# Attention scores as float32r products on the two halves of TensorE's rows

## The reference, cut to what matters

```python
N_HEAD = 16                                   # nh; hs = C // nh = 16
k_eff = (W_dq.T @ W_uq.T @ W_uk).reshape(nh, hs, n_kvl)
c_kv = x @ W_dkv.T
q = (x @ W_dq.T @ W_uq.T).reshape(B, T, nh, hs)
q_lat = jnp.einsum('bqhd,hdl->bhql', q, k_eff)
attn = jnp.einsum('bhql,bkl->bhqk', q_lat, c_kv) / sqrt(hs)
attn = jnp.where(causal[None, None], attn, -jnp.inf)
attn = jax.nn.softmax(attn, axis=-1)
y_lat = jnp.einsum('bhqk,bkl->bhql', attn, c_kv)
y = jnp.einsum('bhql,hld->bqhd', y_lat, v_eff)
```

## Time and profile before

| | before |
|---|---|
| median of 3 runs (lowest, highest) | 1285.98 us (1284.98, 1291.69) |
| the profiled execution | 1286.14 us |
| its span | 1284.0 us |
| PE busy | 91% |
| DVE busy | 67% |
| ACT busy | 52% |
| POOL busy | 30% |
| granted clock of PE, mean | 0.969 |

### The profile page before, as it was taken

One profiled execution on the slowest core, in us unless ns is written; L12 is line 12 of the kernel. 1 busy time (PEld: TensorE's weight loads), 2 busy tenths in 40 slices (PEclk: granted clock), 3 DMA queues, 4 the chain that ended last, 5 costly groups with the idle time before them and its releaser, 6 DMA issues.

```text
span 1284.0 us, 32364 instructions
## 1 busy us (share of the span) xinstructions
PE 1166.2 (91%) x13250; PEld 717.1 (56%) x13250; DVE 857.1 (67%) x2072; ACT 662.6 (52%) x1449; POOL 391.0 (30%) x614
## 2 busy tenths in 40 slices
PE   6889999999999999998799997768899778899995
PEld 3334444444434444433688885436676666688884
DVE  6686868777788888871563367797867563465255
ACT  4446666676666666666432237745554222342232
POOL 5421414141300000002333125645564223643210
PEclk9899999999999999999899998989999999999998
DMA  6754425454564444400000000102111110000003
GB/s 205 165 138 51 88 30 95 59 90 61 90 121 51 51 51 51 51 3 2 1 1 1 1 26 15 31 9 57 38 37 32 40 30 12 3 1 1 1 9 123
DMA packets 78755, 61.65 MB, mean 48 GB/s; under 512 B 41360, under 2 KB 65552, under 8 KB 78480
## 3 DMA queue, kind: packets, MB, share of 16 engines
q1 hardware_dynamic: 77456, 57.18, 24.8%
q10 hardware_dynamic: 1152, 2.41, 0.6%
HBM read 38.20 MB, written 20.97 MB: 46 GB/s over the span
## 4 chain that ended last, share of the span: by engine, by line
PE 32%; DVE 10%; issue 5%; POOL 3%; ACT 1%; DMA 0%; POOLq 0%; DVEq 0%; SPq 0%
PE psum L1044 8%; PE psum L1050 7%; PE psum L1059 2%; PE psum L1588 2%; PE psum L1528 2%; DVE d_products L1725 2%; DVE d_inverse L1730 2%; PE psum L1566 2%; DVE d_conv_sum L1800 1%; PE psum L1557 1%; PE psum L1523 1%; PE psum L1510 1%; PE psum L1514 1%; PE psum L257 1%; PE psum L1537 1%
## 5 line engine op out<-in xcount | busy, mean ns | idle before, releaser
L751 ACT ACTIVATE weights<-psum 128x512 f32<-128x512 f32 (+1 forms) x608 | 318.3, 584 | 156.9 <-PE psum L652 154.8
L652 PE MATMUL psum<-q_stack,k_stack 99*128 99x512 bf16 (+3 forms) x768 | 224.0, 328 | 1.8 <-ACT weights L751 1.0
L574 PE MATMUL psum<-k_stack,q_stack 96*128 96x512 bf16 (+3 forms) x768 | 209.2, 328 | 5.3 <-DVE maxima L809 2.0
L809 DVE TENSOR_REDUCE maxima<-psum 128x1 f32<-128x512 f32 (+2 forms) x304 | 189.2, 683 | 12.5 <-PE psum L574 11.9
L806 DVE CUSTOM_DVE_ANT_0 unread<-psum,mask_scores 128x384 bf16<-128x384 f32 (+1 forms) x256 | 159.5, 623 | 50.3 <-PE psum L574 26.8
L669 PE MATMUL psum<-weights,v_rows 128*17 128x512 f32 (+3 forms) x1536 | 162.0, 494 | 0.1
L545 POOL TENSOR_TENSOR residual<-residual,att_o 128x256 f32<-128x256 f32 x32 | 23.3, 727 | 350.0 <-DVE att_o L842 350.0
L1044 PE MATMUL psum<-f_xT,f_weights_hi 128*128 128x512 f32 x384 | 122.9, 402 | 4.2 <-DVE f_hidden L1160 2.1
L652 PEld LDWEIGHTS psum<-q_stack,k_stack 99*128 99x128 bf16 x768 | 72.6, 98 | 90.1 <-ACT weights L751 41.3
L1086 ACT ACTIVATE f_gates<-psum,ffn_biases 128x512 f32<-128x512 f32 x72 | 49.5, 689 | 140.4 <-PE psum L1050 132.6
L1128 DVE TENSOR_TENSOR f_state<-f_gates 128x512 f32<-128x512 f32 x32 | 27.2, 849 | 116.5 <-POOL f_gates L1003 73.8
(11 more groups left out here) (168 smaller groups left out, 2238.8 us busy)
## 6 DMA issues: line engine op xcount, KB each, us to landing
qk_parts<-a_parts SPq DMA_DIRECT2D x32, 384.0 KB, 3.6
q_stack<-qk_parts SPq DMA_DIRECT2D x90, 128.0 KB, 6.6
k_stack<-qk_parts SPq DMA_DIRECT2D x90, 128.0 KB, 7.3
residual<-in_x SPq DMA_DIRECT2D x8, 512.0 KB, 7.4
out_x<-residual SPq DMA_DIRECT2D x8, 512.0 KB, 3.0
ffn_weights<-in_ffn_w ACTq DMA_DIRECT2D x1, 2048.0 KB, 11.7
systems<-d_attnT_k_kb_v SPq DMA_DIRECT2D x32, 64.0 KB, 1.8
d_systems<-systems SPq DMA_DIRECT2D x4, 512.0 KB, 3.5
```

The source lines that it names most:

```text
L574: m = e.matmul(out[:, i * width:(i + 1) * width], self.qst[st][0:self.ROWS, h, qb * P:(qb + 1) * P], self.kst[st][0:self.ROWS, h, k0:k0 + ...
L652: m = e.matmul(out[:, j * width:(j + 1) * width], self.kst[st][0:self.ROWS + self.MAX_ROWS, h, kb * P:(kb + 1) * P], self.qst[st][0:self.R ...
L751: e.activation(self.weights[n % 2][:, heads[0]:heads[-1] + 1, 0:width], bank[self.score_bank[n, i]][:, 0:len(heads) * width].rearrange("p ...
L809: e.tensor_reduce(to, scores.rearrange("p (h x) -> p h x", h=len(heads)), AXIS_X, ALU.max, negate=True).then_inc(*s["max_red"].did(u, w_at))
```

## The change

Queries and keys are split in two float32r parts instead of three bf16 ones, and three products of them (hi hi, lo hi, hi lo) make a stack of 3 x 16 = 48 rows. Two heads of a unit stand on partitions 0 to 63 of a stack, the other two on 64 to 127, so a head's matmul uses one half of PE's rows. The two halves write different banks. The negated maximum has two parts (50 rows in the second making), and four DMAs. ACT writes hi, DVE (early groups) or POOL (later ones, from a raw copy by ACT) subtracts; the other splitting operations are gone.

A piece for the maxima now takes two adjacent banks, one per half, and DVE reduces both by one instruction: 20 pieces per unit. Every piece and every step on the diagonal is masked on PE, by two bf16 matmuls of 64 rows and 64 columns per head and half; the custom DVE instruction is gone. Scores of one step alternate between the halves (heads 0, 2, 1, 3), steps of 128 columns are two scores of two heads instead of one of four, `mixed` keeps the two of a pair side by side. Scores have banks 0, 1, 6, the ring is 2 to 5, `LEAD` is 6.

```diff
-    SPLIT = ((0, 1, 0, 1, 2, 0), (0, 0, 1, 1, 0, 2))
-    PRODUCTS, ROWS, MAX_ROWS = 6, 6 * HS, 3
-    LEAD = 8
-    PROLOGUE_BANKS, SCORE_BANKS, RING = (0, 1, 2, 3, 4, 5, 6), (0, 1, 2), (3, 4, 5, 6)
+    SPLIT = ((0, 1, 0), (0, 0, 1))
+    PRODUCTS, ROWS, MAX_ROWS, ONES_FROM = 3, 3 * HS, 2, 32
+    HALF, PER_HALF = P // 2, HPU // 2
+    LEAD = 6
+    PROLOGUE_BANKS, SCORE_BANKS, RING = (0, 1, 2, 3, 4, 5, 6), (0, 1, 6), (2, 3, 4, 5)
...
-            self.qst = [sb(f"q_stack{i}", [P, HPU, T], BF16) for i in range(STACKS)]
+            self.qst = [sb(f"q_stack{i}", [P, self.PER_HALF, T], F32R) for i in range(STACKS)]
...
-                n = min(HPU, BANK // width)
-                self.pairs += [(qb, c, width, range(h, h + n)) for h in range(0, HPU, n)]
+                alone = width * self.PER_HALF > BANK
+                self.pieces += [(qb, c, width, heads) for heads in (((0, 2), (1, 3)) if alone else ((0, 1, 2, 3),))]
...
+        self.scored = [((0, 1), (2, 3)) if self.span(n)[1] * self.PER_HALF <= BANK else ((0,), (2,), (1,), (3,))
+                       for n in range(len(self.steps))]
...
+                    size = 2 if item[0] == "max" else 1
+                    while size == 2 and (ring[at % len(ring)] % 2 or ring[at % len(ring)] + 1 not in ring):
+                        at += 1
...
+    def mask(self, e, out, mask, h, heads, width, at):
+
+        k, rows = self.k, self.in_stack(h, self.HALF)[0]
+        columns = out[:, 0:heads * width].rearrange("p (h x) -> p h x", h=heads)
+        for n in range(2):
+            e.matmul(columns[:, :, at + n * self.HALF:at + (n + 1) * self.HALF], k.masks16[rows, mask, n, :],
+                     k.ident16[rows, rows].rearrange("p (o x) -> p o x", o=1).to_broadcast([self.HALF, heads, self.HALF]),
+                     start=n == 0, stop=False, skip_group_check=True)
...
+                for half in range(2):
+                    n = self.PER_HALF * QB
+                    for r in range(self.MAX_ROWS):
+                        row = half * self.HALF + self.ROWS + r
...
+                for half in range(2):
+                    rows, out = self.in_stack(half * self.PER_HALF, self.ROWS)[0], bank[self.bank[item] + half]
+                    if diagonal:
+                        self.mask(e, out, 0, half * self.PER_HALF, each, width, width - P)
+                    for i, h in enumerate(heads[half * each:(half + 1) * each]):
+                        j = h % self.PER_HALF
+                        m = e.matmul(out[:, i * width:(i + 1) * width], self.qst[st][rows, j, qb * P:(qb + 1) * P],
+                                     self.kst[st][rows, j, k0:k0 + width], start=not diagonal and i == 0, stop=True,
+                                     skip_group_check=True)
...
+            for i, h in enumerate(heads):
+                rows, j = self.in_stack(h, self.ROWS + self.MAX_ROWS)
+                m = e.matmul(out[:, i * width:(i + 1) * width], self.kst[st][rows, j, kb * P:(kb + 1) * P],
+                             self.qst[st][rows, j, q0:q0 + width], start=not self.diagonal(n) and i == 0, stop=True,
+                             skip_group_check=True)
...
-                if self.ends_on_diagonal(self.pairs[w_at])[1]:
...
-                    e.tensor_tensor_reduce(self.unread[:, 0:width], scores, k.later16[:, BANK - width:BANK], -1.0, HIGH, ALU.add,
-                                           ALU.min, to).then_inc(*s["max_red"].did(u, w_at))
...
+                e.tensor_reduce(to, k.psum_pairs[self.bank[item] // 2][:, :, 0:each * width].rearrange("p b (j x) -> p b j x", j=each),
+                                AXIS_X, ALU.max, negate=True).then_inc(*s["max_red"].did(u, w_at))
...
-                e.memset(self.kst[st][self.ROWS:self.ROWS + self.MAX_ROWS, :, :], 1.0).then_inc(*s["k_ones"].did(st))
+                    for half in range(2):
+                        at = half * self.HALF
+                        e.memset(self.kst[st][at + self.ONES_FROM:at + self.HALF, :, :].bitcast(F32), 1.0).then_inc(*s["k_ones"].did(st, half))
```

More of the change, by code:

```diff
@@ L319, in __init__ @@
         self.units = [(b, g) for b in range(B) for g in range(UNITS_PER_B)]
-        self.pairs = []
+        self.pieces = []
         for qb in range(QB):
@@ L333, in order @@
     def order(self):
-        per = len(self.pairs)
+        per = len(self.pieces)
         maxima = []
@@ L558, in make @@
             out = bank[self.bank[item]]
-            for w in unmet(self.released[item]):
+            for w in unmet(*self.released[item]):
                 e.wait_ge(*w)
@@ L1907, in constants @@
         (row == col).astype(np.float32),
-        np.where(col > row, np.float32(MASKED), np.float32(0)),
+        *[np.where(later, np.float32(MASKED), np.float32(0))
+          for mask in range(2) for n in range(2) for own in [row % (P // 2) + n * (P // 2)] for later in [own < col if mask else own > col]],
         np.where(ch > row % CH, np.float32(-1), np.float32(0)),
```

187 lines of the change are left out of this document (61 added, 126 removed).

## The result

| | before | after |
|---|---|---|
| median (lowest, highest), us | 1287.87 (1284.98, 1291.69) | 1311.57 (1305.95, 1313.69) |
| span of the profiled execution, us | 1284.0 | 1310.8 |
| PE, DVE, ACT busy | 91%, 67%, 52% | 90%, 62%, 50% |
| granted clock of PE, mean | 0.969 | 0.949 |
| first, last exponential starts, us | 84.9, 607.4 | 86.5, 640.0 |

The changed kernel takes 1.0175 times as long (95% interval 1.013 to 1.022), 24 us more. The forecast was 1266 us, with a range of 1232 to 1304: the time lies above it, and the change went the other way. Executions of one and the same kernel differ in PE's clock: the four of the changed kernel had a mean granted clock of 0.948 to 0.960 and took 1306 to 1314 us, the slowest with the lowest clock.

The account below looks back on a forecast made before the run. PE bounds the kernel; after the change wide steps hang on a score bank and ACT. Terms -10 (late units), -4 (projection units), +2 (last unit), -5 (start) and -3 (idle cover) gave -20: 1266 us from 1286, range 1232 to 1304.

Parts of the forecast that it names:

- The last unit: Last unit of the attention stage: pays first loads and masks with nothing to gain, +2 us.
- Rival D: PE could lose its clock through idle gaps; a tenth of a unit's 20 streamed us is 2: 1296 us, 5%.
- The wide step: Step of four scores without diagonal: 2.78 us with two pieces, 2.54 with one, 2.61 before; no gain on average.
- The chain: In wide steps the fourth score waits for ACT to free the first score's bank, starting 1.16 us after the first.
- float32r: Slower weight loads: 0.08 us on each first product after the V block and on each that waits for a bank.
- Masks: 24 mask blocks per unit and half: 0.20 us from block start to its product, bounds 0.12 and 0.31.
- Bank pairs, and the units with projections: Earlier units with projections: -4 us in all; a single item spoiling a pair costs 0.3 us where a third waits.
- Halves at once, and the reductions: Both halves of PE's rows run together, 7.7 us saved per unit; DVE reductions of 1024 elements take 1.13 us.
- rivals B and C: B: halves' weight loads go one after another, 1303 us, 13%; C: halves don't run at once, 1390 us, 8%.
- Ahead of the units: Before the first unit: first maxima scores 2.5 us earlier and 3 us counted from DVE's saved reductions, -5 us.
- five late units: Late units of the stage: 29.1 us each against 30.5, -1.4, seven times: -10 us.
- The -3 for idle time covered by projections: Projections' cover of PE's idle time, which the forecast thought it took low: -3 us.

Follow-up runs that it names:

- bf16_maxima: Changed kernel with products for the maxima reading the upper two bytes of each float32r value as bf16, scores proper still float32r: 1305.5 us, ratio 1.016.
- no_masks: Changed kernel without any mask matmuls on PE, so part of the computation is missing: 1315.2 us in one execution.
- half_exp: Changed kernel with exponentials of scores of 384 and 512 columns doing only half their columns, part of the computation left out: 1291.9 us in one execution.
- bf16_halves: Changed kernel with stacks, parts and maximum parts in bf16 instead of float32r, which is less precise: 1268.4 us, ratio 0.986 to the kernel before.
- paired_projections: Changed kernel with projections of later tokens two to a step in every fourth step instead of one in every second: 1305.1 us, ratio 1.013.

## Why the prediction was wrong

**The last unit** is the step that failed first. I put +2 us on it, for first loads and masks, and took its clock as full. With the unit ahead of it, where 1.4 us less was forecast, it cost 19.7. The stretches I read for the clock end at 582 us, and the mean of 1.00 there was carried on to a unit of another kind, without pieces between its scores. In the kernel before, the clock was already at half from 587.8 to 591.2, in that very unit, and from 611.7 to 621.9 behind it; the fortieths of the earlier trace rows show 8 and 9 there. At half clock PE is busy 42.7 us of the last unit's 43.5, ACT 20.5. The fourth score of a wide step still waits 0.26 us for its bank, as before; what makes the step longer is PE's own work:

```profile
625.95 0.79 PE L647 MATMUL psum<-q_stack,k_stack 50*128 50x512 f32 x1 [0.26 <-ACT weights L727]
626.67 1.91 PE L663 MATMUL psum<-weights,v_rows 128*17 128x512 f32 x8
```

The V block takes 1.84 us of PE instead of 0.98, and the wide step 4.04 to 4.34 instead of 2.4. Rival D named this (5%), but priced it as a tenth of a unit's time in the middle of the stage, not as a doubling at its end. The same instructions took 32.3 us in bf16_maxima, with 13.7 us at half clock: (43.5 - 32.3) / (43.5 - 13.7) = 0.37 us per us of half clock, so at full clock the last unit would take some 27 us, an estimate from these two, and less than the 28.5 before. By this estimate the whole +15.0 is the clock.

What comes before the falls can be read from all sixteen traces. In the fifteen of the changed kernel and its variants PE waits 1.8 to 2.3 us for the last negated maxima, with no other piece to make meanwhile, and the clock goes to half between 0.5 us before and 1.8 us after that wait ends. The kernel before waits 0.60 us there and keeps its clock:

```profile
583.59 0.27 PE L578 MATMUL psum<-identity,negmax 128*32 128x128 f32 x1 [1.94 <-DVE negmax L784]
```

```profile
574.26 0.27 PE L582 MATMUL psum<-identity,negmax 128*32 128x128 f32 x1 [0.60 <-DVE negmax L814]
584.81 2.74 PE L597 MATMUL psum<-ffn_biases,ffn_weights 128*128 128x1 f32 x24
```

The second line is the 24 one-column matmuls. In eight traces the clock was full when they ended, and it fell 0.2 to 1.5 us later in all eight (in the kernel before at 587.8, 0.2 us after their end); in three more it fell while they ran, two of these with the matmuls moved to step 150; in the other five it was at half already. So a spell follows each of these two. For the 24 matmuls the two runs that moved them bear it out; for the wait it is only seen, not tested. No run removed the wait or spread the 24 matmuls out, so that this would save the time is not shown. How long a spell lasts is open, too: the one behind the wait is 55 us long in this trace although PE is busy 98% of it, 41 in no_masks and 7 to 14 in the other thirteen, with the same instructions in bf16_maxima, and neither rows, nor type, nor order settled it.

**The wide step.** Estimate 2.54 and 2.78 us with one and two pieces, V block of 0.98 included. The step kb 1 (one piece) took 1.70 + 0.98 = 2.68, kb 3 took 2.98. The chain was right in kind (the fourth score starts 1.19 us after the first, 1.16 forecast; half_exp moved it) and right in its main reading, that such steps gain nothing: the four without diagonal even take 8.07 us, V blocks left out, against 7.31. Its size was 0.14 to 0.20 too low, in float32r.

**float32r.** The term was 0.08 us at first products behind V and behind bank waits, 0.08 x (12 + 7) = 1.5 us per unit. Measured: 2.15, late units of bf16_halves against the changed kernel's. What was missed is that a mask in front covers little of a load: 0.10 us at pairs behind masks, too. The Trainium skill, "TensorE: Matmul & The Clock Gate", section "Weight-path perf modes", says that fast weight loading is off for fp32. The traces agree in what they can show, 197 against 96 ns for the mean load. With the figure that the prediction took from that page, 0.5 us more per unit, the estimate would have been 2.0 and nearer.

**Masks.** 0.20 us from block to product were forecast; it is 0.07, as before, and 0.15 with the longer record of the product behind it. All masks together cost about 1 us per unit in no_masks, 0.04 for each of the 24 blocks, since many stand in steps that something else bounds. The term was too high, and helped to hide the others.

**Bank pairs, and the units with projections,** are the second step that failed: -4 us were forecast and +12.3 came, 10.6 of it at full clock. I gave 0.3 us to a third item that spoils a pair. The wait behind the turned maxima alone is 0.70 us, and kb 5 is 0.79 above its forecast (2.69 against 1.90). From 86 to 366 us PE waited 4.9 us for such reductions and 4.6 for copies of projections, some 16 us in all, where the kernel before waited 0.6 (86 to 358):

```profile
PE psum L429 <- DVE negmax L779: 4.9, 7, 0.7
PE psum L429 <- ACT a_parts L715: 3.2, 5, 0.7
PE psum L570 <- ACT a_parts L715: 1.4, 4, 0.4
```

Those units got 1.3 us longer instead of 0.5 shorter. That the broken pairs are the cause is argued from these waits; paired_projections, which was to show it, left the units as long and the waits as they were. My test was whether DVE has the time. It has (139.9 of 183 us, 23.3 per unit; 22.7 forecast). What counts is how far ahead PE may run: a ring of four banks held four pieces before, and holds two now.

**Halves at once, and the reductions** were right: pairs start 0.01 us apart, so rivals B and C fall, and 1024 elements take 1.16 us (forecast 1.13). (Two readings of the forecast were a little off: 36 times 512 columns at 0.22 are 7.9 us, not 7.7, and the first step before took 2.08, not 2.16. Neither matters to the sum.) Two tiles that share all columns load their weights side by side. The Trainium skill, "TensorEngine Tiling (Array Packing)", section "Key Properties", calls tiles independent, and the trace agrees; the drain at a change of tiling mode that it names can't be told from the rest here: from the V block to the next scores it is 0.98 us as before.

**Ahead of the units** -5 us were forecast, and it was +1.5. The first maxima scores came at 36.28 against 37.41, 1.1 us earlier and not 2.5. What they waited for is the stack's load:

```profile
36.28 0.27 PE L429 MATMUL psum<-identity,mask_scores 64*128 64x128 bf16 x3 [1.34 <-DMA k_stack<-qk_parts]
38.55 0.30 PE L429 MATMUL psum<-identity,mask_scores 64*128 64x128 bf16 x4 [1.75 <-DVE a_parts L769]
```

The second line and one more of 0.79 us are waits for DVE's subtraction, 2.5 us in two; the kernel before had three of 2.2 in all, so this is no new cost. What differs is the clock: PE was at half for 20.4 us ahead of the first exponential, and for 13.8 before (38.2 to 48.5, 65.5 to 69.0), which can cost up to 3.3 us.

Of the sum -20: five late units -1 and the last but one +5 for -10, units with projections +12 for -4 (up to 3.4 of it in a spell of half clock), start +1.5 for -5, last unit +15 for +2. The -3 for idle time covered by projections has no counterpart; PE waits more there, not less. Behind the stage, where nothing was forecast, it is -5.8.

## What to carry to other kernels

When a change takes work from PE, ask for every stretch, the last and thinnest above all, what it would cost at half clock, and read the clock of the kernel before in that stretch, not its mean over the busy ones. Reductions over two banks at once halve the number of things under way in a ring of the same size: count how far PE can run ahead, and what a single-bank item does to a pair, before counting DVE's time. In the last stretch look also for what a spell follows: here a wait of 2 us for the last reduction, and a run of one-column matmuls. Float32r weights took 0.10 us more per pair behind a 70 ns mask: a short matmul does not hide a long load. And before a trace is taken to show that an edit moved the clock, look at variants that leave that stretch alone; here their last unit took 32 to 37 us, and 43.5 in the changed kernel.

## What the runs showed of the hardware

- Two tiles of 50 rows each that share all 128 columns run at once, with their weight loads: starts 0.01 us apart, 0.50 us for both products of 512 columns.
- A float32r operand read as bf16 through every second element of two bytes is no slower than a packed one to within the reading: 0.23 us for a pair of 512 columns against 0.21 to 0.22, and late units got shorter by it (29.72 us against 30.45).
- Taking work out need not shorten the whole: no_masks has 1 us less per late unit and took 1315.2, against 1306 to 1314 with masks; PE's clock was at half for 61 of the 65 us from 567.8 to 632.6 in that one trace.
- PE can be busy 98% of 50 us (590 to 640) and be granted 0.50 of its clock throughout. It is not bound to be: the same last unit had half clock for 13.7 of 32.3 us in bf16_maxima.
- The clock fell at the end of a PE wait of 1.8 to 2.3 us in fifteen of fifteen traces, and within 1.5 us of the end of 24 one-column matmuls in all eight in which it had been full until then.
